# Order of the weighted cross sum, the query projections and DVE's block writes in a decoder layer on one core

## The reference

```python
    x = _layernorm(x + attn(x, ...), axis=-1)          # self attention, softmax over keys
    q = (x @ Wq.T + bq).reshape(b, s, 16, 64)
    k = (ctx @ Wk.T + bk).reshape(b, s, 16, 64)
    v = (ctx @ Wv.T + bv).reshape(b, s, 16, 64)
    scores = jnp.einsum('bshd,bsgd->bshg', q, k) * inv_sqrt_dk
    attn = jax.nn.softmax(scores, axis=-1)
    out = jnp.einsum('bshg,bsgd->bshd', attn, v)
    out = jnp.transpose(out, (0, 2, 1, 3)).reshape(b, -1, 16 * 64)
    x = _layernorm(x + out @ Wo.T + bo, axis=-1)
    x = _layernorm(x + ffn(x, ...), axis=-1)
```

## Time and profile before

| | |
|---|---|
| median of 3 runs | 464.46 us (462.92 to 466.68) |
| profiled execution | 465.74 us |
| its span in the trace | 463.9 us |
| granted TensorE clock, mean | 0.98 |
| busy: PE, DVE, ACT, POOL | 409.9 (88%), 292.0 (63%), 243.6 (53%), 146.4 (32%) us |

### The profile page before, as it was taken

The page is one execution under the profiler, slowest core; times in us unless marked ns, Lnnn a source line. Parts: engine busy times, 40 slices in busy tenths (PEclk is TensorE's granted clock), DMA queues, the critical chain, the costliest instruction groups (busy, mean ns, idle before and its releaser), DMA issues.

```text
span 463.9 us, 15115 instructions
## 1 busy us (share of the span) xinstructions
PE 409.9 (88%) x6068; PEld 354.7 (76%) x6068; DVE 292.0 (63%) x655; ACT 243.6 (53%) x828; POOL 146.4 (32%) x218
## 2 busy tenths in 40 slices
PE   7769799999899978999998959998998999898893
PEld 6568678788788867787887858787887878677673
DVE  2653787775847774766837764767767766726334
ACT  2684646554665353744656343764637466436331
POOL 5030416150422442331414351421514262403022
PEclk9989999999999998999999998999999999989997
DMA  7800201210100112110101112100101010101002
GB/s 241 310 2 1 50 11 45 62 42 1 35 21 19 37 36 68 24 30 7 40 10 30 31 36 68 32 16 8 45 10 35 20 47 15 35 18 30 24 1 69
DMA packets 43599, 19.28 MB, mean 42 GB/s; under 512 B 36544, under 2 KB 40896, under 8 KB 43536
## 3 DMA queue, kind: packets, MB, share of 16 engines
q1 hardware_dynamic: 42688, 16.88, 13.5%
q0 software_dynamic: 560, 1.38, 0.9%
q10 hardware_dynamic: 288, 0.07, 0.1%
HBM read 8.88 MB, written 1.05 MB: 21 GB/s over the span
## 4 chain that ended last, share of the span: by engine, by line
PE 60%; ACT 12%; DVE 11%; issue 5%; SPq 5%; POOL 4%; DMA 3%; POOLq 0%; DVEq 0%; ACTq 0%
ACT p L497 8%; PE ps L920 6%; PE ps L1072 6%; PE ps L1019 6%; PE ps L1097 5%; SPq L313 4%; PE ps L1138 4%; PE ps L900 4%; PE ps L973 4%; PE ps L901 3%; PE ps L902 3%; POOL p L387 3%; PE ps L949 3%; PE ps L940 3%; DVE neg_max L709 3%
## 5 line engine op out<-in xcount | busy, mean ns | idle before, releaser
L497 ACT ACTIVATE p<-ps,neg_max 128x128 f32<-128x128 f32 x256 | 89.8, 382 | 59.2 <-DVE neg_max L709 59.2
L387 POOL TENSOR_TENSOR p<-p,row_inv 128x1024 f32<-128x1024 f32 x32 | 60.7, 1896 | 88.7 <-DVE row_inv L791 76.5
L490 ACT ACTIVATE pt<-ps 128x512 f32<-128x512 f32 x64 | 35.4, 602 | 47.7 <-PE ps L1019 47.7
L497 ACT ACTIVATION_READ_ACCUMULATOR p<-ps,neg_max 128x1 f32 x256 | 57.5, 225 | 0.0
L1019 PE MATMUL ps<-ident,p 128*128 128x128 f32 x256 | 37.2, 294 | 16.8 <-issue 8.6
L1019 PEld LDWEIGHTS ps<-ident,p 128*128 128x128 f32 x256 | 30.8, 150 | 21.7 <-issue 13.1
L1138 PE MATMUL ps<-x1t,wq 128*64 128x64 f32 x1024 | 36.8, 225 | 7.8 <-ACT x1t L559 7.8
L709 DVE TENSOR_REDUCE neg_max<-ps 128x4 f32<-128x512 f32 x64 | 42.0, 680 | 0.2 <-PE ps L1123 0.2
L1138 PEld LDWEIGHTS ps<-x1t,wq 128*64 128x64 f32 x1024 | 33.0, 138 | 11.5 <-DVE pt L661 8.4
L740 DVE TENSOR_TENSOR ot<-ps,bv 128x512 f32<-128x512 f32 x32 | 22.0, 689 | 25.9 <-PE ps L1072 25.8
L377 POOL TENSOR_TENSOR ve<-mv,eps 128x1 f32<-128x1 f32 x16 | 3.0, 189 | 107.7 <-DVE mv L761 107.7
(11 more groups left out here) (138 smaller groups left out, 860.2 us busy)
## 6 DMA issues: line engine op xcount, KB each, us to landing
v<-v2s SPq DMA_DIRECT2D x256, 32.0 KB
xg<-x_t SPq DMA_DIRECT2D x4, 256.0 KB, 2.7
pt<-w_qk SPq DMA_DIRECT2D x4, 256.0 KB, 8.3
cg<-ctx_t SPq DMA_DIRECT2D x4, 256.0 KB, 3.2
wo<-w_o SPq DMA_DIRECT2D x2, 512.0 KB, 9.3
out<-x2b SPq DMA_DIRECT2D x4, 256.0 KB, 2.2
xres<-x_nat SPq DMA_DIRECT2D x15, 64.0 KB, 1.8
bv_row<-b_v POOLq DMA_DIRECT2D x1, 512.0 KB, 9.5
```

The source lines that it names most:

```text
L387: nc.gpsimd.tensor_tensor(ph, ph, row_inv[:, 8 * half:8 * half + 8].unsqueeze(2).to_broadcast([T, 8, T]), ALU.mult).then_inc(p_ready, 1)
L490: nc.scalar.activation(pt[:, u * BANK:(u + 1) * BANK], bank(T_BANK[u]), ACT.Copy).then_inc(pt_ready, 1)
L497: last = nc.scalar.activation(p[:, hd * T:(hd + 1) * T], bank(S_BANK[q])[:, pos * T:(pos + 1) * T], ACT.Exp, bias=neg_max[:, hd:hd + 1], a ...
```

## The change

On DVE the second spread moves from behind the second maximum to directly behind the first spread, and x1 moves ahead of the first maximum; the four maxima then follow each other. On PE `weighted_v2(s, 1)` moves from behind `project_q2(0)` to directly behind `weighted_v2(s, 0)`, and `project_q2(1)` directly behind `project_q2(0)`; in step 16, where pieces of the feed-forward block stand between them, these keep their places relative to each other. ACT, POOL and SP are not touched.

```diff
@@ DVE, step @@
                     block_diagonal(s, 0)
-                if a:
-                    score_max(0)
+                    block_diagonal(s, 1)
                 if bc:
                     dve.wait_ge(rs1_ready, s)
                     nc.vector.tensor_scalar(x1[:], t1[:], mv1[:, 0:1], rs1[:, 0:1], ALU.subtract, ALU.mult).then_inc(x1_ready, 1)
                 if a:
+                    score_max(0)
                     score_max(1)
-                if d:
-                    block_diagonal(s, 1)
-                if a:
                     score_max(2)
                     score_max(3)
@@ PE, step @@
                     weighted_v2(s, 0)
+                    weighted_v2(s, 1)
                 if ffn:
...
                     pe.wait_ge(x1t_ready, s)
                     project_q2(0)
-                if d:
-                    weighted_v2(s, 1)
+                    project_q2(1)
                 if ffn:
                     down(0, 1)
                     up(0, 3)
-                if bc:
-                    project_q2(1)
                 if ffn:
                     down(0, 2)
                     up(0, 4)
```

## The result

The changed kernel is slower: median 473.74 us of 4 runs (471.64 to 476.06) against 465.31 of 4 runs of the kernel before on the same chip, ratio 1.0188 (95% interval 1.0121 to 1.0254). Six more runs of the same program, timed later against 23 of the kernel before, gave 471.27 against 463.84, ratio 1.0147 (1.0103 to 1.0190). So the change costs 1.5 to 1.9%, where 1.1% was forecast. The sign was right. The size was not: the measured time is above the range. Ratios and intervals are those on record, which leave out three slow runs of the kernel before and are not the quotients of the medians beside them (these would be 1.018 and 1.016 here, and 1.040 for e3).

A forecast was written before the change was run, and what follows sets the result against it. No engine alone was the bound: each batch is a relay, PE holding 60% of the chain. Waits of +6.8 us and clock of -1.7 gave +5.1, so 469.6 us on the median, 1.1% slower; range 465.5 to 472.5.

The forecast's parts named there:

- The relay, +6.8: All steps: later maximum 0 delays x1t, projections and DVE's copy; the delays reaching the end sum to +6.8 us.
- phases 3 and 0: Steps 3, 7, 11 late by 0.69 each, 2.1 us; steps 4, 8, 12 by 0.82 each, 2.5 us.
- the short steps: Steps 2, 5, 9, 13, 14, 15: PE's delay fits into its wait for POOL's division; 0.07 each, 0.4 us.
- The cover: PE's wait for POOL's division, 0.66 or 0.9 from its last weight load, said to absorb PE's 0.82 us.
- Step 1: No weighted sum here; maximum 0 falls behind x1, so ACT's exponentials come 1.03 later: +1.0 us.
- The jumps move with PE: Loop returns after steps 6 and 10: the wait starts with PE's branch, passing on 0.82 us each, 1.6 in all.
- the jumps do not move with PE: Rival at the loop returns: the wait there absorbs 0.75 us each, giving 468.1 us; chance 0.11.
- Step 16 and its clock: Step 16: earlier moves of v2 bring x1 forward, -0.85 us, and its clock fall goes, -1.7 us.
- the clock term, −1.7: Step 16: PE's shorter idle time ends the fall to 1.2 GHz, -1.7 us; bounds 0 and -1.7.
- The clock stays as in step 16: Rival: the clock falls in step 16 as before, so the full 6.8 us remain, 471.3 us; chance 0.27.
- Absorbed: Rival: following steps absorb the delay, half of the 4.6 us of phases 0 and 3 going, 467.3 us; chance 0.11.
- The change does what it is for: Rival: the second weighted half fills PE's wait for x1t, saving up to 7.8 us, 456.7 us; chance 0.06.

The follow-up runs named there:

- e3: DVE's new order with PE's old one, against the kernel before: 482.56 us, ratio 1.0362.
- e7: PE's new order, DVE's maxima and spreads as before, DVE's regrouping copy directly behind the maxima, against the kernel before: 454.52 us, ratio 0.9836.
- e2: The changed kernel run again without any edit, against the kernel before: 471.27 us, ratio 1.0147.
- e4: PE's new order with DVE's old one, against the kernel before: 461.10 us, ratio 0.9936.
- e5: The changed kernel with DVE's regrouping copy moved from behind q2_out(0) to directly behind the four maxima: 468.32 us, ratio 1.0118 to the kernel before.
- e8: The changed kernel, but in step 1 DVE takes maximum 0 ahead of x1 as before: 468.75 us, ratio 1.0129 to the kernel before.
- e6: The changed kernel with the x1t copy ahead of exponentials(0) on ACT: 466.82 us, ratio 1.0069 to the kernel before.
- e1: The kernel before run again without any edit: 463.30 us of 12 runs, ratio 0.9993.

## Why the prediction was right in part and missed the size

**The relay, +6.8: right, at 7.2.** For the steps of phases 3 and 0 it had 2.1 and 2.5; measured 3 x 0.65 = 2.0 and 3 x 0.78 = 2.3. For the short steps it had 0.07 each and the table shows 0.14. The cover was taken at 0.9, but the whole of it was the 0.66 of the earlier trace rows: 0.82 − 0.66 = 0.16. In the changed kernel the first transposition behind step 9 starts right behind the cross scores, with no wait left:

```profile
259.41 1.16 PE L1195 MATMUL ps<-kb,qt 64*64 64x64 f32 x64
260.50 1.77 PE L1016 MATMUL ps<-ident,p 128*128 128x128 f32 x12
```

Step 1 had +1.0 and showed 1.08 and 1.43, of which up to 0.4 is the clock. The two returns had 1.6, for the delay that the jump passes on, and step 16 had -0.85 and showed -0.44. The sum is 2.3 + 2.0 + 0.7 + 1.0 + 1.6 - 0.4 = 7.2, near the 7.3 us between the means that do not go with the clock.

**The jumps move with PE: right.** PE's timeline at the second return, the kernel before, then the changed one:

```profile
272.18 1.16 PE L1200 MATMUL ps<-kb,qt 64*64 64x64 f32 x64
```

```profile
279.27 1.16 PE L1195 MATMUL ps<-kb,qt 64*64 64x64 f32 x64
284.91 1.32 PE L1016 MATMUL ps<-ident,p 128*128 128x128 f32 x5 [4.48 <-issue]
```

The cross scores start 6.97 after x1 before (x1 of step 10 at 265.21) and 7.75 in the changed kernel (x1 at 271.52). From there to the first transposition it is 5.32 and 5.64, at the first return 5.57 in both, and between 5.32 and 6.15 at all 20 returns of the ten profiles, in e7 too (5.38 and 5.35), whose cross scores come at x1 + 6.30. Had the restart been tied to another engine's work, this gap would have shrunk by 0.8 in the changed kernel. The gap scatters, though, and that is a term too: e2 has 6.15 and 5.82, 1.1 more in sum than the kernel before, and this is a part of its 2.30 and 2.29. The rival "the jumps do not move with PE" falls. By the rule of the Trainium skill (Runtime: NRT & Kernel Launch, Instruction fetch mechanics), that a taken branch out of the instructions at hand fetches its target first, the wait starts with the branch. The trace agrees, and it has the fetch, which the prediction took for something that no run shows: around PE's pause at the second return of the kernel before, from 273.00 to 277.50, two packets start in the DMA queue that the profile calls instruction (packets, MB, share of 16 engines):

```profile
q8 instruction: 2, 0.03, 3.9%
```

All 20 returns have such a pair, started within 1.5 us of each other, and outside the returns no two packets of that queue start within 2.5 us of each other in any of the ten profiles.

**Step 16 and its clock: right in the sum, with some luck.** The prediction took −0.85 for x1 and −1.7 for the clock, together −2.55. Measured: x1 of step 16 gains 0.44 on the rest, and behind it another 2.07 goes (the changed kernel is 9.70 late at that x1 and 7.63 at the last copy of the weighted sum), together −2.51. The two misses, 0.4 each, cancel. The 2.07 is also more than the 1.7 that the fall can cost (3.4 us at half clock); what the rest is was not taken apart. That the larger part belongs to the fall is borne out by e3, in which the fall stays and the stretch behind x1 changes by 0.02, and by e4, e5, e7 and e8, in which it is gone and the stretch is shorter by 2.06 to 2.08. The changed timeline:

```profile
411.68 1.29 DVE L751 TENSOR_TENSOR v2s<-ps,bv_row 128x512 f32<-128x512 f32 x2
...
415.88 0.34 DVE L769 TENSOR_SCALAR x<-t,mv,rs 128x128 f32<-128x128 f32 x1
...
416.37 0.30 PE L1129 MATMUL ps<-perm,x 128*128 128x128 f32 x1 [0.90 <-DVE x L769]
```

The wait for the DMA (2.13 in the earlier trace rows) is gone, PE stands 0.90 instead of 1.80 ahead of x1's transposition, and the window from 414 to 422 has clock 1.00 where the earlier trace rows had 0.79:

```profile
414.00:422.00 8.00, 7.10 (x151) 5.86 (x150) 3.40 (x8) 4.52 (x6) 1.19 (x3) 1.00 0.09 23
```

**The step that failed: the clock term, −1.7 as the whole of it.** It counted the fall that goes and no fall that comes or grows. Two do. Two of its readings helped to hide this. The stretch of the earlier trace rows, named for waits that go by at clock 1.00, has no wait in it: PE is busy for 19.40 of 19.40 us (behind the 15 waits for `x1t` the trace has no fall, so the claim itself holds). And 1.80 and 4.16 were not the only idle times to look at: PE's wait of 3.19 at the start of step 1 was followed by a fall at 32.2, and one of 1.93 at 15.5 by none.

In step 1 the prediction named the risk ("the wait of step 1 grows to 2.0 and could bring a new fall, most of which the 1.13 of wait behind it would take"), and left it out of the sum. The fall came: `x1t` comes after 2.00 of wait, and the projections, 2.08 in step 9, take 3.62:

```profile
51.48 3.62 PE L1135 MATMUL ps<-x1t,wq 128*64 128x64 f32 x64 [2.00 <-ACT x1t L559]
```

That is 1.5 us longer; the wait behind it took all but 0.4 of it (1.43 against the forecast 1.0) in one profile and nearly all in e2 (1.08).

At the returns the prediction had no clock term. PE restarts there with a stretch at clock 0.50, which is 1.2 GHz. The windows of the two stretches, before:

```profile
175.60:179.00 3.40, 3.08 (x15) 3.09 (x16) 0.00 (x0) 1.43 (x3) 1.26 (x3) 0.50 0.28 50
278.00:281.40 3.40, 3.40 (x16) 3.21 (x15) 0.00 (x0) 2.40 (x5) 0.68 (x2) 0.50 0.23 55
```

And after:

```profile
177.90:184.70 6.80, 4.88 (x20) 4.59 (x21) 1.32 (x6) 2.69 (x5) 2.03 (x4) 0.50 0.39 99
284.00:290.40 6.40, 5.49 (x21) 5.11 (x22) 0.75 (x3) 3.19 (x6) 1.44 (x4) 0.50 0.38 105
```

PE works 3.1 and 3.4 us at half clock before, 4.9 and 5.5 after. Of that extra work half its length is lost time: (4.9 − 3.1)/2 + (5.5 − 3.4)/2 = 1.95. The returns show 1.62 + 2.12 = 3.74 of increase, 2.1 over the forecast 1.64, so these 1.95 are nearly all of it.

Whether the edit makes this stretch longer is not shown. Four returns of the changed kernel have the long one and four of the kernel before the short one, but these are two executions of each, and e7, with PE earlier than before, has one of each. The time at 1.2 GHz of all executions differs by less (3.7 us) than that of the profiled ones (5.0 by the same formula). What the executions show without the profiles is the sign: the clock adds 1.3 us where the forecast had -1.7, and these 3.0 are most of the 3.5 by which the means lie further apart than the forecast.

The account of the profiled execution: forecast +5.1; phases 3 and 0 −0.3, the short steps +0.3 (0.72 for 0.4), step 1 +0.4, the returns +2.1, step 16 nothing: +7.6, and the span is 471.5 − 463.9 = 7.6 longer. In the profiles the gap between forecast and result is the clock at the returns, with a little of step 1.

**The rivals.** "The clock stays as in step 16" (0.27) was wrong about step 16 and closest in time, for another reason. "Absorbed" falls: every phase 0 and phase 3 distance carries its delay. "The change does what it is for" falls for the change as a whole, but its mechanism is real: it names the length of the moved half against the lateness of `x1t`, and where `x1t` is not made late (e4, e7) the kernel is faster, 1.6% in e7. The forecast's two named culprits, the late `x1t` and the DVE copy behind L702, are each confirmed by an experiment that takes one away (e6, e5).

## What to carry to other kernels

In a relay written out by hand, an edit on two engines is two edits: measure each alone. Here PE's part gains 0.6%, DVE's loses 3.6%, and PE's part with one DVE copy moved up gains 1.6%. Before a producer is moved up, read what its engine and the next one now do later; ahead of every wait that is to be filled, ask who else reads the block that fills it. And where a stall changes length or place, the clock behind it is a term of the sum of its own, with a sign that can differ from stall to stall.

## What the runs showed of the hardware beyond the forecast

- **The low stretch at a return of the loop comes in two lengths.** In the 20 returns of the ten profiles the granted clock goes to 0.50 for either 3.4 or 6.8 us. It was 6.8 us in the twelve returns in which it fell 1.1 to 2.0 us ahead of PE's restart, and 3.4 in the eight in which it fell within 0.4 ahead of the restart or up to 0.7 after it. The changed kernel had the long one at all four returns seen, the kernel before the short one at all four, and e5 and e7 one of each. What sets where the fall lies was not found: PE's idle time ahead of the restart is 4.2 to 4.9 us with the short stretch and 4.2 to 5.0 with the long one. A short one of e7, from its windows:

```profile
271.40:274.70 3.30, 3.30 (x17) 3.20 (x16) 0.00 (x0) 2.04 (x4) 0.76 (x2) 0.50 0.23 55
```

- **The length of a stall does not tell alone whether the clock falls.** Waits of 2.00 us in step 1 (four profiles) and of 1.80, 1.87 and 2.01 in step 16 (the kernel before, e3, e1) each go with a fall, which begins between 0.5 us before the end of the wait and 1.0 after it; up to 0.98 and 1.33 in the same two places there is none. But e3 has a fall behind a wait of 1.27 for `x1t` and none behind ten others of 1.27 to 1.70, and a wait of 3.19 at the start of step 1, the same in all ten profiles, is followed by a fall in seven and by none in three (e4, e5, e8).
- **Two executions of one single-core program differ by up to 6.6 us** (461.28 to 467.92 in e1), with mean clocks from 0.970 to 0.979, and the first step starts up to 4 us earlier or later in the span. Distances between the steps of the loop, its returns apart, repeat to 0.04 us and are what a small change should be read from.
